# A two-layer attention and mixture-of-experts kernel on one core: front blocks' numbers in loads of six registers, all dummy rows on the sync queue, ScalarE's activations ahead of its copies, the second group's ranks moved back

## The reference

```
x = x + softmax_attention(layernorm(x), ctx)        # 16 heads, layer 0
x = x + moe0(layernorm(x))                          # 8 experts, top 2, silu(g) * v, hidden 256
x = x + linear_attention(layernorm(x), ctx)         # softmax over head features of q and k
x = x + moe1(layernorm(x))                          # 8 experts, top 2, gelu, hidden 512, + 2 shared experts
```

## Time and profile before

| what | value |
|---|---|
| median of 3 runs | 716.31 us (714.04 to 717.26) |
| the profiled execution | 716.5 us, of which 714.5 us is the span of the records |
| PE busy | 655.3 us, 92% of the span |
| DVE, ACT, POOL busy | 452.1, 340.4, 383.2 us |
| granted TensorE clock, mean | 0.966 of full speed |
| the chain that ended last | PE 65%, DVE 14%, SP's queue 5%, "issue" 5%, ACT 4%, DMA 3%, POOL 2% |

### The profile page before, as it was taken

The page is one execution under the profiler, slowest core; times in us unless marked ns, Lnnn a source line. Parts: engine busy times, 40 slices in busy tenths (PEclk is TensorE's granted clock), DMA queues, the critical chain, the costliest instruction groups (busy, mean ns, idle before and its releaser), DMA issues.

```text
span 714.5 us, 15805 instructions
## 1 busy us (share of the span) xinstructions
PE 655.3 (92%) x5160; PEld 494.1 (69%) x5160; DVE 452.1 (63%) x1336; ACT 340.4 (48%) x739; POOL 383.2 (54%) x502
## 2 busy tenths in 40 slices
PE   6999999999998879999998899999998799999991
PEld 3556666665667669899997455556554599999990
DVE  2577788788877757786778568776564133333433
ACT  3444454454443244444666466766543354544440
POOL 5312255765746744555677566676645145545552
PEclk9999999999999689999999999999999999999997
DMA  6831112112210167888882300000001888888875
GB/s 178 238 61 11 8 20 30 34 19 29 36 26 24 55 174 220 248 260 265 253 262 84 100 31 27 23 30 27 31 21 52 237 272 261 264 261 268 278 232 165
DMA packets 102120, 91.36 MB, mean 128 GB/s; under 512 B 52952, under 2 KB 85848, under 8 KB 101720
## 3 DMA queue, kind: packets, MB, share of 16 engines
q1 hardware_dynamic: 88487, 69.85, 35.4%
q0 software_dynamic: 8640, 17.84, 7.1%
q10 hardware_dynamic: 4913, 2.67, 1.4%
HBM read 69.14 MB, written 22.72 MB: 129 GB/s over the span
## 4 chain that ended last, share of the span: by engine, by line
PE 65%; DVE 14%; SPq 5%; issue 5%; ACT 4%; DMA 3%; POOL 2%; POOLq 0%; DVEq 0%; ACTq 0%
PE pair L1543 37%; PE pair L1877 11%; PE pair L1546 8%; PE pair L1941 5%; DVE sm L1272 4%; DVE smax L1268 4%; PE pair L1668 2%; PE pair L1683 2%; DMA xr<-xs_sorted 1%; SPq L500 1%; SPq L504 1%; POOL xs_sorted L615 1%; SPq L493 1%; ACT L924 1%; SPq L494 1%
## 5 line engine op out<-in xcount | busy, mean ns | idle before, releaser
L689 POOL DMA_INDIRECT y_tok<-ysb,xr x142 | 138.8, 978 | 123.7 <-DVE ysb L1149 58.5
L615 POOL DMA_INDIRECT xs_sorted<-xa,slot_i x128 | 131.5, 1027 | 86.2 <-DVE slot_i L1055 50.9
L1543 PE MATMUL pair<-xT,w_all 128*128 128x256 f32 (+1 forms) x640 | 139.3, 362 | 0.0
L1543 PEld LDWEIGHTS pair<-xT,w_all 128*128 128x128 f32 x640 | 109.7, 196 | 9.6
L1877 PEld LDWEIGHTS pair<-w_all,hT 128*128 128x128 f32 x852 | 107.6, 194 | 6.0 <-issue 2.8
L1877 PE MATMUL pair<-w_all,hT 128*128 128x128 f32 x852 | 109.3, 277 | 2.2 <-DVE hT L1135 1.9
L873 ACT ACTIVATE hT<-pair,w_all 128x256 f32<-128x256 f32 (+1 forms) x160 | 62.5, 448 | 74.5 <-PE pair L1543 73.8
L1127 DVE COPY xT<-pair 128x256 f32<-128x256 f32 (+1 forms) x80 | 31.4, 393 | 95.2 <-PE pair L1546 91.5
L937 ACT ACTIVATE hS<-pair,w_sh 128x512 f32<-128x512 f32 x64 | 44.0, 687 | 60.5 <-PE pair L1543 59.7
L1543 PE MATMUL pair<-xeT_all,w_sh 128*128 128x512 f32 x128 | 68.6, 619 | 0.0
L1941 PE MATMUL pair<-hS,w_sh 128*128 128x512 f32 x128 | 66.4, 602 | 0.0
(11 more groups left out here) (222 smaller groups left out, 1090.3 us busy)
## 6 DMA issues: line engine op xcount, KB each, us to landing
w_all<-in_w SPq DMA_DIRECT2D x40, 578.0 KB, 4.3
w_all<-in_w SPq DMA_DIRECT2D x40, 450.0 KB, 3.9
xa<-y_tok SPq DMA_DIRECT2D x32, 256.0 KB, 4.3
xr<-xs_sorted SPq DMA_DIRECT2D x62, 130.0 KB, 3.3
y_tok<-ysb,xr POOLq DMA_INDIRECT x142
xs_sorted<-xa,slot_i POOLq DMA_INDIRECT x128, 2.3
xs_sorted<-in_pads SPq DMA_DIRECT2D x12, 130.0 KB, 3.9
xr<-xs_sorted SPq DMA_DIRECT2D x18, 65.0 KB, 2.6
```

What stands on the lines that cost most here:

```text
L615: g.indirect_dma_start(xs_dram[l], bass.IndirectOffsetOnAxis(ap=slot_i[:, i:i + 1], axis=0), xa[:, GT * c + j // TOPK, j % TOPK, :], None)\
L689: g.indirect_dma_start(y_dram[l], bass.IndirectOffsetOnAxis(ap=xr[u % NXR][:, t, P:P + 1].bitcast(I32), axis=0), ysb[u % NYB][:, t, :], None)\
L1543: return mm(out_, l_, r_, start=True, stop=True)
```

## The change

Seven edits.

1. At the head of `routed`, SP reads the 5 experts, 6 first rows and 6 counts of the front blocks in three loads into 5, 6 and 6 registers, and then issues weights and rows back to back. The 8 places of the dummy rows come in one load as well.
2. SP issues all 8 dummy-row transfers; ScalarE's three, in both layers, go.
3. ScalarE in `routed(0)`: `up(u)`, then `gate_rows(u-2)`, then `beside(u)`.
4. `shared_step`: unit 1 does 10 half-steps instead of 8 (places 0, 2, 3, 4, 5, 8, 9, 12, 13 carry work; place 1 has none), and from unit 2 on every half-step comes two places earlier, so unit 9 ends with fewer.
5. In unit 1 TensorE's `out_turned`, `project` and `column_sums` stand elsewhere and `ranks(1, 0)` goes to the end of the unit; `project(1)` waits for the logits of group 0, which share its bank (`lg_ready` counts on through both layers for this).
6. In unit 8 `shared_turn(6)` goes behind half-step 13 and `list_order(1)`.
7. VectorE adds the bias of layer 1 (L1408) ahead of the last three `context_shift`.

```diff
 def shared_step(u, k):
-    at = (k if k % 2 else k // 2) if u == 1 else 16 * (u - 1) - 8 + k
-    return divmod(at, 2) if u > 1 or k % 2 == 0 else (-1, 0)
+    at = 16 * (u - 1) - 6 + k
+    if u == 1:
+        at = {0: 0, 1: 1, 2: 2, 3: 3, 4: 4, 5: 5, 8: 6, 9: 7, 12: 8, 13: 9}.get(k, -1)
+    return divmod(at, 2)
...
                 sp.wait_ge(S("tails"), l + 1)
-                for k in range(0, E - 3):
-                    tail_rows(k)
+                _, ends = nc.values_load_multi_w_load_instructions(tail_i[0:1, 0:E], engines=[sp.engine], min_val=0,
+                                                                   max_val=(E - 1) * PITCH + NTOK)
+                for k in range(E):
+                    sp.dma_start(xs_dram[l][bass.ds(ends[k], P), :], a["pads"][k * P:(k + 1) * P, :])\
+                        .then_inc(S("xs_padded"), 16)
                 sp.wait_ge(S("emap"), l + 1)
                 sp.wait_ge(S("blocks_padded"), 16 * 2 * -(-SPARE // BLK))
+                _, first_e = nc.values_load_multi_w_load_instructions(e_i[0:1, 0, 0:NWB], engines=[sp.engine], min_val=0, max_val=E - 1)
+                _, first_r = nc.values_load_multi_w_load_instructions(e_i[0:1, 1, 0:AHEAD], engines=[sp.engine], min_val=0,
+                                         max_val=E * PITCH + SPARE - 2 * P)
+                _, first_n = nc.values_load_multi_w_load_instructions(e_i[0:1, 2, 0:AHEAD], engines=[sp.engine], min_val=1, max_val=3)
                 for k in range(AHEAD):
                     if k < NWB:
-                        block_weights(u0 + k)
-                    block_rows(u0 + k)
+                        block_weights(u0 + k, first_e[k])
+                    block_rows(u0 + k, first_r[k], first_n[k])
...
-                for k in range(E - 3, E):
-                    tail_rows(0, k)
...
                     for u in range(NB + 2):
-                        beside(u)
+                        if u < NB:
+                            up(u)
                         if u >= 2:
                             gate_rows(u - 2)
-                        if u < NB:
-                            up(u)
+                        beside(u)
...
                 context_shift(4)
                 list_rows(0)
-                for g in range(5, NGRP):
-                    context_shift(g)
...
                 v.tensor_tensor(bias[:, 5, :], bank[5][:, 0:P], bias[:, 5, :], ALU.add).then_inc(S("bias1_ready"), 1)
+                for g in range(5, NGRP):
+                    context_shift(g)
...
             def project(u):
                 pe.wait_ge(S("oT_ready1"), u + 1)
+                if u == 1:
+                    pe.wait_ge(S("lg_ready"), NGRP + 1)
...
                     if u > 1 and live(u):
                         values(u)
+                    if u == 1:
+                        out_turned(u)
                     fill(8, 9)
                     if u == 1:
-                        out_turned(u)
+                        project(u)
                     if live(u - 1):
                         after(pe, S("sx_added"), u - 2)
                         column_sums(1, u - 1)
                     fill(10, 11)
                     if u > 1 and live(u):
                         out_turned(u)
-                    if u == 1:
-                        project(u)
-                    if live(u - 1):
+                    if u > 1 and live(u - 1):
                         ranks(1, u - 1)
                     fill(12)
                     if u > 1 and live(u):
                         project(u)
-                    if live(u - 2):
+                    if live(u - 2) and u != NGRP:
                         shared_turn(u - 2)
                     fill(13)
                     if u == NGRP:
                         list_order(1)
+                        shared_turn(u - 2)
                     fill(14)
                     if u == NGRP:
                         list_smalls(1)
                     fill(15)
+                    if u == 1:
+                        ranks(1, u - 1)
```

More of the change, by code:

```diff
@@ L489, in routed, with block_weights, block_rows @@
                 wc = (W0C, W1C)[l]
-                def block_weights(u):
+                def block_weights(u, e=None):
                     after(sp, S("y_sum"), u - NWB + 1)
-                    e = sp.value_load(e_i[0:1, 0, u - u0:u - u0 + 1], min_val=0, max_val=E - 1)
+                    if e is None:
+                        e = sp.value_load(e_i[0:1, 0, u - u0:u - u0 + 1], min_val=0, max_val=E - 1)
                     sp.dma_start(w_blk[u % NWB][:, 0:wc], wsrc[bass.ds(e, 1)].rearrange("o p c -> p (o c)"))\
                         .then_inc(S(f"w_in{u % NWB}"), 16)
-                def block_rows(u):
+                def block_rows(u, r=None, count=None):
                     after(sp, S(f"y_out{u % NYB}"), stored(u - NXR + NYB))
                     n = tiles_of(u)
-                    r = sp.value_load(e_i[0:1, 1, u - u0:u - u0 + 1], min_val=0, max_val=E * PITCH + SPARE - n * P)
+                    if r is None:
+                        r = sp.value_load(e_i[0:1, 1, u - u0:u - u0 + 1], min_val=0, max_val=E * PITCH + SPARE - n * P)
                     if u == u0 + NFRONT:
                         sp.wait_ge(S(f"rows{l}"), TOPK * 16 * (NT - GT))
+                    if u < u0 + NEARLY_B and count is None:
+                        count = sp.value_load(e_i[0:1, 2, u - u0:u - u0 + 1], min_val=1, max_val=3)
                     if u < u0 + NEARLY_B:
-                        count = sp.value_load(e_i[0:1, 2, u - u0:u - u0 + 1], min_val=1, max_val=3)
                         sp.wait_ge(S("sorted"), count)
@@ L748, in norm_input @@
                 last.then_inc(S(f"xn_ready{l}"), 1)
-            def tail_rows(l, k):
-                act.wait_ge(S("tails"), l + 1)
-                r = act.value_load(tail_i[0:1, k:k + 1], min_val=0, max_val=(E - 1) * PITCH + NTOK)
-                act.dma_start(xs_dram[l][bass.ds(r, P), :], a["pads"][k * P:(k + 1) * P, :]).then_inc(S("xs_padded"), 16)
             def context_values(g):
@@ L957, in attention1 @@
                     gelu(u, 2)
-                    if u == NGRP + 1:
-                        tail_rows(1, 5)
                     if live(u) and u > 1:
@@ L965, in attention1 @@
                     gelu(u, 4)
-                    if u == NGRP + 1:
-                        tail_rows(1, 6)
                     if live(u) and u > 1:
@@ L972, in attention1 @@
                         second_copy(u - 1)
-                    if u == NGRP + 1:
-                        tail_rows(1, 7)
                     if live(u + 1):
@@ L1285, in logits @@
                     v.tensor_copy(lg[:, GT * u:GT * (u + 1), :], bank[logit_bank(u)][:, 0:GT * E].rearrange("p (t e) -> p t e", e=E))\
-                        .then_inc(S("lg_ready0"), 1)
-                    dve.wait_ge(S("lg_ready0"), u + 1)
+                        .then_inc(S("lg_ready"), 1)
+                    dve.wait_ge(S("lg_ready"), u + 1)
                 def output(u):
@@ L1459, in logits @@
                 dve.wait_ge(S("logit_done1"), u + 1)
-                link(v.tensor_tensor(lg[:, GT * u:GT * (u + 1), :],
-                                     line_bank("logits", u)[:, 0:GT * E].rearrange("p (t e) -> p t e", e=E),
-                                     rb[:].unsqueeze(1).to_broadcast([P, GT, E]), ALU.add))
+                v.tensor_tensor(lg[:, GT * u:GT * (u + 1), :],
+                                line_bank("logits", u)[:, 0:GT * E].rearrange("p (t e) -> p t e", e=E),
+                                rb[:].unsqueeze(1).to_broadcast([P, GT, E]), ALU.add).then_inc(S("lg_ready"), 1)
+                dve.wait_ge(S("lg_ready"), NGRP + u + 1)
             def output(u, steps=(0, 1)):
@@ L1695, in expand @@
                     if u != U_LAST:
-                        after(pe, S("lg_ready0"), u)
+                        after(pe, S("lg_ready"), u)
                     for t in range(GT):
```

3 lines of the change are left out of this document (removed).

## The result

The changed kernel takes 737.89 us (median of 4 runs, 737.12 to 738.06) against 716.21 us of the kernel before (4 runs, 714.04 to 717.26): ratio 1.0305, 95% interval 1.028 to 1.033, so 21.7 us slower. Forecast were 724.8 us and a range of 716 to 731. The direction was right, the size was not. The profiled execution spans 735.9 us against 714.5, 21.4 more.

What follows compares the result with a forecast made beforehand. PE was taken as the bound in every stage but the turn-overs. Terms -3.5 (front, layer 0), +1.8 (ScalarE's order), +2.5 (unit 1), +11.3 (half-step 9), -3.8 (front, layer 1) gave +8.3: 716.5 to 724.8 us, range 716 to 731.

Steps and rivals of the forecast that it cites:

- I take 3 us, a load mostly and 0.1 for each further value.: SP's three loads of 17 values ahead of the first weights: 3 us, so these leave 2.4 us later.
- The bound that I had given, 10 us: Cost of SP's 17 values if the price is all in the value; 1.8 us if all in the load.
- What the fronts win back: Block rows and weights at both layers' heads come faster behind the first weights; net -3.5 us (layer 0), -3.8 (layer 1).
- the limit named in advance: Layer 0: the fourth front block's rows cannot leave before the `sorted` signal at 263.58; 2.0 us taken by the seventh block.
- Values are dear: Rival, chance 0.05: at 0.6 us a value the first weights leave 9 us late in both layers; 740 us.
- Half-step 9: Units 2 to 8: PE's first `shared_down` of a group waits 1.62 us for `shared_out`, seven times, +11.3 us.
- Hidden half-step 9: Rival, chance 0.12: the wait moved to half-step 9 is hidden as at 11; the rest gives -3.0, 713.5 us.
- The low clock: Rival, chance 0.06: each 1.62 us gap in units 2 to 8 lowers PE's clock, 7 x 1.6 us more, 736 us.
- ScalarE's order: `routed(0)`: silus and copies ahead of `beside` delay steps 29, 32, 39 and others, win at step 40; sum +1.8 us.
- Unit 1: `attention1`: one more chunk; idle time moves to `expert_turned(1)`, some 3.7 us; +1.6 and 0.9 for low clock, +2.5 us.
- The moved chunk: The chunk moved into unit 1 counts only at the other end of `attention1`, which is bound by the list.
- the dummy rows cost nothing: SP's extra dummy rows end before the list is ready and cost nothing.

Runs made afterwards that it cites:

- e2: The changed kernel with 22 of the 34 range checks left out, those of block and row numbers: 729.45 us, ratio 1.0207 to the kernel before.
- e5: The changed kernel with ScalarE's `shared_out` put ahead of both the four normalisations and the gelu of half-step 8: 725.31 us, ratio 1.0121 to the kernel before.
- e3: The changed kernel with ScalarE's `shared_out` put ahead of the gelu of half-step 8 only: 730.75 us, ratio 1.0201 to the kernel before.
- e4: The changed kernel with ScalarE's old order in `routed(0)` (beside, copies, silus): 734.79 us, ratio 1.0273 to the kernel before.
- e6: The kernel before with only the change's `attention1` part (`shared_step`, unit 1's order, `ranks`, `shared_turn`, `lg_ready` signals): 725.35 us, ratio 1.0142.
- e10: The kernel before with only the range checks of block number and row number left out: 711.16 us, ratio 0.9925.
- e1: The changed kernel with the list read block by block again, nothing read ahead, SP's eight dummy rows kept: 731.64 us, ratio 1.0231 to the kernel before.
- e7: The kernel before with ScalarE's silus ahead of `beside` in step 39 of `routed(0)` alone: 717.14 us, ratio 1.0018.

## Why the prediction was wrong

- **The step that failed: "I take 3 us, a load mostly and 0.1 for each further value."** The three loads cost no more than that (0.64 to 0.8 each, 1.9 to 2.4 together), but each value also brings its two checks, 0.27 to 0.29 us and 4.5 to 5.0 for the 17, which I had counted in the order's rows (34 instructions on registers) and left at nothing. From the list to the first weights it is 6.35 and 6.83 us more than before at the two heads instead of 2.4; of the 6.83, 0.5 is SP's dummy rows. The bound that I had given, 10 us, held it; the value taken was at the wrong end. The earlier trace rows could have told it: a load with its two register instructions is 0.6 and a transfer with its one 0.5, which nowhere says that register instructions are free.
- **What the fronts win back.** Behind the first weights the pace of 1.1 us a block wins back 4.6 us of 6.8 in layer 0 (+2.2) and 3.2 of 8.6 in layer 1 (+5.4), where the 8.6 are how much later the first weights leave against the end of `attention1`, 1.7 of them the chunk that moved. The forecast needed 5.9 and 5.0, so this term was high by 1 to 2 us as well; the price of the values is the larger error. In layer 1 part of it is a slip: the 2.3 us a block are the weights' bytes alone, while the 2 us of layer 0 had the rows in them. With the rows (66.6 kB) it is 2.5 us at 260 GB/s, and the term is 1.1 instead of 2.0. e2 shows the limit named in advance, the `sorted` signal.
- **Values are dear** was the right rival in kind: 9 us late (6.8 measured), 740 us (737.9 measured). Its price of 0.6 a value was too high (7.29 us for 17 is 0.43), and the 4 us that it took from each head were 2.2 and 5.4, so that the sum came this near is in part luck. I gave it 5 of 100; between bounds of 1.8 and 10 us with no row of a load of several registers that was far too little, and the range stopped short of it.
- **Half-step 9 was right**, with its cause and nearly its size: 1.61 us start to start against 1.62, 1.69 by the length of the unit, 11.8 for 11.3. e5 takes it away. What I missed is that the gelu is only one of two things ahead of `shared_out`; the normalisations hide behind it (e3). *Hidden half-step 9* is dismissed by the seven waits.
- **The low clock did not come**: a wait of 1.45 us seven times leaves the clock at 1.00 from 420 to 574 us; the 0.99 of the stretch from 410 us on has the wait of 3.48 in it. The rule of the Trainium skill (TensorE: Matmul & The Clock Gate, A second HAM failure mode) does not show here at gaps of this length and this distance. That the clock fell behind 385.22 in the trace of before, on which the rival was built, is not what every trace shows: in e4 and e6 it stayed at 1.00 behind the same wait; and in e10 it fell behind the wait of 1.76 in unit 8, behind which it stayed high before.
- **ScalarE's order**: 1.70 and 1.70 at steps 32 and 39 (1.8 and 1.7 forecast), 1.12 more at step 29 (1.0), 1.86 between (1.1), and 3.31 back at step 40 (3.8): +3.1 for +1.8. Of the 3.31, 1.7 is the low clock of the kernel before, forecast at 1.6; against a trace without it (e4, e6) the order costs 4.7. What made the term too small is thus the steps between (1.86 for 1.1) and the give-back, and its second part hangs on the execution. The exp waits show no drain at the table load: by the rule of the Trainium skill (ScalarE: Activation LUTs, What ACT_TABLE_LOAD costs) each would have been 1.38 longer than 1.70, as an estimate; in step 32 the load starts 0.01 us after the copies end and the exp 0.02 after the load.
- **Unit 1**: `expert_turned(1)` waits 3.48 for `keep_input`, forecast 3.7. But before, PE waited 0.89 for `high`, 2.27 for the column sums and 0.91 for `xeT_all` in this unit and the start of the next; now it waits 0.87 for `lent` and 0.23 for the column sums there and not for `xeT_all`. And a stretch of low clock, for which I added 0.9, is there in both kernels, so the sum is +0.2 for +2.5.
- **The moved chunk** costs the heads of layer 1 little cover (e6: 0.3 us at the end). That the dummy rows cost nothing holds for layer 0; in layer 1 they keep SP past the list and cost 0.5 to 0.6 us (e1, and the changed kernel, 7.81 for 7.29). Their move alone was not tried, nor was VectorE's earlier bias.

## What to carry to other kernels

Price a read of numbers into registers by what stands in the instruction list: here each value with a stated range brought two checks of 0.13 to 0.15 us each, and loading many at once saved only the smaller part; anything read ahead of the first transfer is paid before it, so read what that transfer needs and no more. When an instruction of a saturated engine moves earlier, look at everything ahead of its supplier in the supplier's own order, not just at the nearest entry. And time won ahead of a stage that is bound by a chain through other engines is waited away there.

## What the runs showed of the hardware

- With two silus, two copies and a table load of 1.28 us ahead of it on ScalarE, the exp of a step takes PE's wait from 0 to 1.70 us; between these rows there is no further gap.
- On SP a range check of a value costs 0.13 to 0.15 us, a load of one register about 0.3 and a load of five or six 0.64 to 0.8 (worked out from the table above).
- Behind the same wait of 1.9 us TensorE's clock fell in the traces of before (0.57 from 386 to 390 us) and e10 (0.72 from 379 to 385), and stayed at 1.00 in those of e4 and e6. Behind the wait of 1.76 in unit 8 it stayed high before and fell in e10, to 0.50 from 541 to 544 us. One trace does not tell what such a wait costs.
- The path from the list to the first weights is longer in layer 1 than in layer 0 for the same instructions: 7.81 against 7.29 us in the changed kernel, 5.09 against 4.05 in e2. The loads need not be dearer for this: SP is busy with its dummy rows until 571.10 there, 1.0 after the list, and until 566.40 in e2, 1.1 after it; from then on it is 6.8 and 4.0.
- The kernel before varied from 711.8 to 722.8 us over its runs, more than the 0.5% on which the forecast's chances were built; differences under 2 us needed the rows. Part of this lies in the attention of layer 0: its clock from 0 to 225 us is 0.98 in the trace of before and 1.00 in that of e7, whose code is the same there, and the list comes 3.2 us earlier in e7.
